# Step input of a state-space scan: scaled by B along the partitions and turned into PSUM, with the sums as accumulating transposes

## Chip, cores and metric

One core of one Trainium2 chip. The metric is device time in microseconds (us) of one execution of the whole program, a decoder layer; smaller is better. TensorE, VectorE, ScalarE, GpSimd and SyncE are PE, DVE, ACT, POOL and SP in the rows.

## What is computed

The change lies in the first of the layer's stages, a selective scan over 32 sequences of 128 tokens with 256 channels and 16 states. Attention, a mixture of experts and a last layer norm follow and stay as they are.

```python
x_dbl = jnp.einsum('bld,ed->ble', hidden_states, W_xproj)   # 64 + 16 + 16 columns
dt_low, Bm, Cm = x_dbl[..., :64], x_dbl[..., 64:80], x_dbl[..., 80:]
delta = softplus(jnp.einsum('blr,dr->bld', dt_low, W_dt) + b_dt)
dA = jnp.exp(delta[..., None] * A)
dBx = (delta * x)[..., None] * Bm[:, :, None, :]
h = dA_t * h + dBx_t                    # for every token t, state n, channel d
y = jnp.einsum('bdn,bn->bd', h, C_t)
x = _layernorm(x + y, axis=-1)
```

## The kernel before

The stage is `scan_phase`. It takes the 32 sequences in 8 groups of 4 (GROUPS, GB), 512 tokens (GT) in a row along the free axis, with the 256 channels as KH = 2 halves of 128 partitions. Inside a group it takes the 16 states one after the other; one state is called a step, so the stage has 128 steps (q = 16 g + n). Each engine has a hand-written program of its own that loops over the groups and steps, and the engines meet at semaphores only.

One step n, with k for the two channel halves:

- ACT, `decays` (L358): decay = exp(A_n * delta), two instructions, made two steps ahead.
- The drive, delta * x * B_n, goes to the PSUM tiles `drive_ps[k]`, one per half. In 12 of 16 steps DVE makes it itself, `drives` (L452): dx from PSUM times `b_sb`, B's row n copied to all 128 partitions. In the steps of POOL_STEPS (2, 6, 9, 14) POOL makes it in SBUF, `make_drive` (L523), and ACT copies it over, `copy_drive` (L366).
- DVE, `scan` (L463): state = decay * previous + drive along the 512 tokens, one instruction per half.
- POOL, `outputs` (L538): hc = state * C_n, both halves in one instruction; C_n is also a row that was copied to all partitions.
- PE, `add_state` (L256), three steps later: y_ps[k] += hc[k], a product with the identity.

SP loads the two broadcast rows of each step (`load_b`, L189, and `load_c`, L196; 128 loads of 256 KB each). State, decay, hc and the rows live in rings of 4 slots (RING), so the scan of step q waits until hc of step q - 4 is made, and a decay waits until the scan four steps back is done.

While one group runs, the next is prepared: PE projects x (`project`, L240 and L242, then `step_size`, L249), ACT takes the parts of the softplus (L333 to L344), POOL adds them to delta (L509) and multiplies by x (L516), ACT copies dx to PSUM (L352). A group's sum comes out with the channels on the partitions; it is copied (`copy_y`, L371), turned by PE (`turn`, L274), and normalised over the channels (DVE L470 and L476, POOL L528 and L531, ACT L384) during the next group.

What sets the order is the code as written, for each engine alone; on ACT a step is:

```python
decays(par, q + 2, n + 2)
if n + 1 in POOL_STEPS:
    copy_drive(g, n + 1)
```

Of the kernel before, what the change touches and what calls it, by code (L numbers as in the profile page):

```python
# [35 lines left out]
POOL_STEPS = (2, 6, 9, 14)  # L36


def merge_moments(dve, stats, stats_ready, stats_count, part, mean, var, done, before):

    even, odd = stats[:, :, 1], stats[:, :, 4]
    dve.wait_ge(stats_ready, stats_count)
    dve.tensor_tensor(part[:, 0, :], even, odd, ALU.add)
    dve.tensor_tensor(part[:, 1, :], even, odd, ALU.subtract)
    dve.tensor_tensor(part[:, 2, :], stats[:, :, 2], stats[:, :, 5], ALU.add).then_inc(done, 1)
    dve.wait_ge(done, 3 * before + 1)
    dve.tensor_scalar(mean[:], part[:, 0, :], 0.5, None, ALU.mult)  # L50
    dve.scalar_tensor_tensor(part[:, 3, :], part[:, 1, :], 0.25, part[:, 1, :], ALU.mult, ALU.mult).then_inc(done, 1)
    dve.wait_ge(done, 3 * before + 2)
    dve.scalar_tensor_tensor(var[:], part[:, 2, :], 1.0 / D, part[:, 3, :], ALU.mult, ALU.add).then_inc(done, 1)
# [20 lines left out]
def scan_phase(nc, x1, ident, xT_dram, w_proj_dram, w_bc_dram, w_dt_dram, b_dt_dram, a_log_dram, bc_dram, attention):  # L74
    with ExitStack() as ctx:
        s = Scope(nc, ctx, "scan")
        w_proj = s.sb("w_proj", [P, KH, R])
        w_bc = s.sb("w_bc", [P, KH, 2 * NS])
        w_dt = s.sb("w_dt", [R, D])
        b_dt = s.sb("b_dt", [P, KH])  # L80
# [4 lines left out]
        rows = s.sb("rows", [2 * NS, GT])  # L85
        dt_low = s.sb("dt_low", [R, GT])
# [3 lines left out]
        z_pos = s.sb("z_pos", [P, KH, GT])  # L90
        delta = [s.sb(f"delta{i}", [P, KH, GB, SEQ]) for i in range(2)]
        dx = [s.sb(f"dx{i}", [P, KH, GT]) for i in range(2)]
        drive = s.sb("drive", [P, KH, GT])
        decay = s.sb("decay", [P, RING, KH, GB, SEQ])
        state = s.sb("state", [P, RING, KH, GT])
        b_sb = s.sb("b_sb", [P, RING, GT])
        c_sb = s.sb("c_sb", [P, RING, GT])
        hc = s.sb("hc", [P, RING, KH, GT])
        yT = s.sb("yT", [P, KH, GT])
        stats = s.sb("stats", [P, GB, 6])  # L100
        moment = s.sb("moment", [P, GB, 2])
        scaled = s.sb("scaled", [P, GB])
        shift = s.sb("shift", [P, GB])
        zero = s.sb("zero", [P, GB])
# [12 lines left out]
        zeroed = s.sem("zeroed")  # L117
        a_ready = s.sem("a_ready")
        proj_ready = s.sem("proj_ready")
        dt_copied = s.sem("dt_copied")  # L120
        rows_ready = s.sem("rows_ready")
        rows_stored = s.sem("rows_stored")
        b_loaded = [s.sem(f"b_loaded{i}") for i in range(RING)]
        c_loaded = [s.sem(f"c_loaded{i}") for i in range(RING)]
        z_ready = s.sem("z_ready")
# [3 lines left out]
        z_pos_ready = s.sem("z_pos_ready")  # L129
        delta_ready = s.sem("delta_ready")  # L130
        dx_ready = s.sem("dx_ready")
        dx_copied = s.sem("dx_copied")
        decay_ready = s.sem("decay_ready")
        drive_ready = s.sem("drive_ready")
        drive_made = s.sem("drive_made")
        drive_copied = s.sem("drive_copied")
        scanned = s.sem("scanned")
        hc_ready = s.sem("hc_ready")
        hc_summed = s.sem("hc_summed")
        y_started = s.sem("y_started")  # L140
        y_copied = s.sem("y_copied")
        turned = s.sem("turned")
        stats_ready = s.sem("stats_ready")
        stats_seen = s.sem("stats_seen")
        mv_ready = s.sem("mv_ready")
        scaled_ready = s.sem("scaled_ready")
        shift_ready = s.sem("shift_ready")
        lv_ready = s.sem("lv_ready")
        rstd_ready = s.sem("rstd_ready")
        normed = s.sem("normed")  # L150
        consts = 4

        def pool_drives(g, n):
            return len(POOL_STEPS) * g + len([x for x in POOL_STEPS if x <= n])

        def dve_drives(g, n):
            return KH * ((STEPS - len(POOL_STEPS)) * g + len([x for x in range(n + 1) if x not in POOL_STEPS]))

        def slot_use(g, n):
            return 16 * (STEPS // RING * g + n // RING + 1)  # L160

        with nc.Block() as block:

            @block.sync
            def _(sp):
                sp.dma_start(w_proj[:], w_proj_dram).then_inc(proj_loaded, 16)
                sp.dma_start(w_bc[:], w_bc_dram).then_inc(proj_loaded, 16)
                sp.dma_start(xT[0][:], xT_dram[:, :, 0:GT]).then_inc(x_loaded[0], 16)
                sp.dma_start(w_dt[:], w_dt_dram).then_inc(const_loaded, 16)
                sp.dma_start(b_dt[:], b_dt_dram).then_inc(const_loaded, 16)  # L170
                sp.dma_start(a_log[:], a_log_dram).then_inc(const_loaded, 16)
                sp.dma_start(ident[0][:], ident[1]).then_inc(const_loaded, 16)

                def store_rows(i, par):
                    g = 2 * i + par
                    sp.wait_ge(rows_ready, g + 1)
                    sp.dma_start(bc_dram[par], rows[:]).then_inc(rows_stored, 16)

                def load_b(i, par, n, first=False):
                    g = 2 * i + par  # L180
                    if n == 0:
                        sp.wait_ge(rows_stored, 16 * (g + 1))
                    if not first:
                        back, m = (g, n - RING) if n >= RING else (g - 1, n - RING + STEPS)
                        if m in POOL_STEPS:
                            sp.wait_ge(drive_made, pool_drives(back, m))
                        else:
                            sp.wait_ge(drive_ready, dve_drives(back, m))
                    sp.dma_start(b_sb[:, n % RING, :], bc_dram[par, n:n + 1, :].broadcast_to([P, GT])).then_inc(b_loaded[n % RING], 16)  # L189

                def load_c(i, par, n):
                    g = 2 * i + par
                    if n == 0:
                        sp.wait_ge(rows_stored, 16 * (g + 1))
                    sp.wait_ge(hc_ready, STEPS * g + n + 1)
                    sp.dma_start(c_sb[:, n % RING, :], bc_dram[par, NS + n:NS + n + 1, :].broadcast_to([P, GT])  # L196
                                 ).then_inc(c_loaded[n % RING], 16)

                def group(i, par, fetch, final=False):
                    g = 2 * i + par  # L200
                    for n in range(STEPS):
                        if n == STEPS - RING - 1 and not final:
                            store_rows(i + par, 1 - par)
                        ahead = n + RING
                        if ahead < STEPS:
                            load_b(i, par, ahead)
                        elif not final:
                            load_b(i + par, 1 - par, ahead - STEPS)
                        ahead = n + RING - 1
                        if ahead < STEPS:  # L210
                            load_c(i, par, ahead)
                        elif not final:
                            load_c(i + par, 1 - par, ahead - STEPS)
# [100 lines left out]
            def _(act):  # L314
# [116 lines left out]
                for n in range(2):  # L431
                    decays(0, n, n)
# [1525 lines left out]
```

## Time and profile before

| | |
|---|---|
| median of 3 timed runs | 1349.92 us (1348.81 to 1350.81) |
| span of the profiled execution, first to last instruction (its own time is given as this span alone) | 1350.7 us |
| first scan starts, last scan starts | 26.0 us, 474.0 us |
| busy in the whole program: PE, DVE, ACT, POOL | 1037.0, 953.6, 713.6, 863.4 us |
| scan stage, 26.0 to 475.2 us: PE, DVE, ACT, POOL busy | 320.00, 413.91, 262.95, 401.78 us of 449.20 |

Busy time of an engine in a stretch counts overlapping instructions once; the mean ns of an instruction is its own length, of which about a tenth of a microsecond overlaps the next where two follow without a wait. A line number is the line of the kernel's source. "Idle before" is how long the engine stood still ahead of an instruction, with the instruction that released it.

### The profile page before, as it was taken

The page shows a single profiled execution, that of the slowest core. Times are in us where ns is not written, and L with a number is a line of the kernel's source. Part 1 is how long each engine was busy: PE and PEld are TensorE (multiplying, and loading weights), DVE is VectorE, ACT ScalarE, POOL GpSimd, SP SyncE. Part 2 cuts the span into 40 slices and gives each one's busy share as a digit, 9 for nine tenths or more (in the row PEclk, how much of TensorE's full clock was granted, in tenths as well). Part 3 has the DMA queues.
Part 4 walks back from the last instruction along what each step waited for, and adds up shares of the span by engine and source line. Part 5 has one row for each costly group of instructions (what it writes and reads, how often), then busy time and mean ns, then how long its engine had stood idle before and what let it go on. Part 6 is the DMA issues. An engine that isn't in the chain of part 4 may idle for free. (4 is left out here: it accounts for less than half of the span.)

```text
span 1350.7 us, 25649 instructions
## 1 busy us (share of the span) xinstructions
PE 1037.0 (77%) x8275; PEld 713.5 (53%) x8275; DVE 953.6 (71%) x1824; ACT 713.6 (53%) x1537; POOL 863.4 (64%) x762
## 2 busy tenths in 40 slices
PE   4877577775767758888888886127999999999980
PEld 1332222322223236666666665026989898999970
DVE  2998999989899947777777875674555555555534
ACT  4565565664656425666666663113555555555433
POOL 4898988989889846777777774405244463464423
PEclk8898998989989869999999997557999999999995
DMA  5454544545444300111111110104243443343317
GB/s 177 149 165 142 176 141 158 169 142 177 144 163 156 127 26 21 45 39 35 35 46 37 35 37 25 70 1 137 48 106 72 115 89 70 103 96 76 40 20 260
DMA packets 80620, 130.71 MB, mean 97 GB/s; under 512 B 12656, under 2 KB 38832, under 8 KB 78512
## 3 DMA queue, kind: packets, MB, share of 16 engines
q1 hardware_dynamic: 68272, 112.91, 25.2%
q0 software_dynamic: 12288, 17.05, 7.8%
q8 instruction: 32, 0.52, 0.2%
q14 instruction: 28, 0.23, 0.1%
HBM read 108.26 MB, written 21.66 MB: 96 GB/s over the span
## 5 line engine op out<-in xcount | busy, mean ns | idle before, releaser
L538 POOL TENSOR_TENSOR scan_hc<-scan_state,scan_c_sb 128x1024 f32<-128x1024 f32 x128 | 298.9, 2356 | 46.8 <-PE scan_y_ps L256 33.9
L463 DVE TENSOR_TENSOR_SCAN scan_state<-scan_decay,scan_drive_ps 128x512 f32<-128x512 f32 x256 | 296.4, 1202 | 33.8 <-ACT scan_drive_ps L366 26.3
L256 PE MATMUL scan_y_ps<-scan_hc,all_ident 128*128 128x512 f32 x524 | 252.8, 623 | 63.4 <-POOL scan_hc L538 63.4
L1624 POOL DMA_INDIRECT acc<-expert_rows,input_lst x64 | 111.2, 1737 | 180.4 <-DVE expert_rows L1753 165.7
L1727 DVE TENSOR_TENSOR expert_hid_lo<-expert_hid,expert_hid_hi 128x512 fp32r<-128x512 f32 x128 | 88.6, 692 | 172.0 <-ACT expert_hid_hi L1711 172.0
L256 PEld LDWEIGHTS scan_y_ps<-scan_hc,all_ident 128*128 128x128 f32 x524 | 96.8, 195 | 212.6 <-POOL scan_hc L538 109.0
L1706 ACT ACTIVATE expert_hid<-expert_h_ps,expert_b 128x512 f32<-128x512 f32 x128 | 88.2, 689 | 189.3 <-PE expert_h_ps L588 187.2
L358 ACT ACTIVATE scan_decay<-scan_delta,scan_a_neg 128x508 f32<-128x508 f32 x256 | 165.0, 710 | 9.4 <-DVE scan_state L463 6.8
L586 PE MATMUL expert_o_ps<-weights_w_hi,expert_hid_hi 128*128 128x256 f32 x512 | 143.9, 281 | 2.2 <-DVE expert_hid_lo L1727 2.2
L588 PE MATMUL expert_o_ps<-weights_w_hi,expert_hid_lo 128*128 128x256 f32 x512 | 143.8, 281 | 0.0
L587 PE MATMUL expert_o_ps<-weights_w_lo,expert_hid_hi 128*128 128x256 f32 x512 | 143.4, 280 | 0.0
L452 DVE TENSOR_TENSOR scan_drive_ps<-scan_dx_ps,scan_b_sb 128x512 f32<-128x512 f32 x192 | 122.1, 682 | 12.0 <-ACT scan_dx_ps L352 12.0
L586 PE MATMUL expert_h_ps<-expert_x_hi,weights_w_hi 128*128 128x512 f32 x256 | 106.6, 416 | 2.4 <-DVE expert_x_lo L1739 2.4
L588 PE MATMUL expert_h_ps<-expert_x_hi,weights_w_lo 128*128 128x512 f32 x256 | 102.1, 399 | 0.0
L587 PE MATMUL expert_h_ps<-expert_x_lo,weights_w_hi 128*128 128x512 f32 x256 | 102.0, 398 | 0.0
L586 PEld LDWEIGHTS expert_o_ps<-weights_w_hi,expert_hid_hi 128*128 128x128 f32 x512 | 96.5, 188 | 8.3 <-issue 2.6
L587 PEld LDWEIGHTS expert_o_ps<-weights_w_lo,expert_hid_hi 128*128 128x128 f32 x512 | 96.6, 189 | 5.9
L588 PEld LDWEIGHTS expert_o_ps<-weights_w_hi,expert_hid_lo 128*128 128x128 f32 x512 | 96.8, 189 | 0.0
L1241 POOL DMA_INDIRECT input_xg<-table,input_lst x64 | 71.4, 1115 | 27.4 <-issue 16.8
L1066 DVE TENSOR_REDUCE attn_top<-attn_s_ps 128x4 bf16<-128x512 f32 x128 | 84.0, 678 | 3.8 <-PE attn_s_ps L839 3.7
L1711 ACT ACTIVATE expert_hid_hi<-expert_hid 128x512 fp32r<-128x512 f32 x128 | 79.5, 621 | 0.6
L366 ACT ACTIVATE scan_drive_ps<-scan_drive 128x512 f32<-128x512 f32 x64 | 37.2, 600 | 75.9 <-DVE scan_state L463 75.9
(215 smaller groups left out, 2327.2 us busy)
## 6 DMA issues: line engine op xcount, KB each, us to landing
scan_b_sb<-rows SPq DMA_DIRECT2D x128, 256.0 KB, 3.6
scan_c_sb<-rows SPq DMA_DIRECT2D x128, 256.0 KB, 3.4
weights_w<-w SPq DMA_DIRECT2D x16, 1024.0 KB, 5.2
table<-all_row SPq DMA_DIRECT2D x32, 132.0 KB, 1.7
scan_xT<-xT SPq DMA_DIRECT2D x8, 512.0 KB, 4.5
attn_ctxT<-ctxT SPq DMA_DIRECT2D x32, 128.0 KB, 2.4
acc<-all_row SPq DMA_DIRECT2D x32, 128.0 KB, 1.7
final_a<-acc SPq DMA_DIRECT2D x8, 512.0 KB, 6.6
```

Of the source, the lines that this page charges most:

```text
L256: last = pe.matmul(y_ps[k][:], ident[0][:], hc[:, n % RING, k, :], start=False, stop=(n == NS - 1))
L358: act.activation(decay[:, n % RING, k, :, 1:SEQ], delta[par][:, k, :, 1:SEQ], ACT.Exp, scale=a_neg[:, k, n:n + 1]).then_inc(decay_ready, 1)
L452: dve.tensor_tensor(drive_ps[k][:], dx_ps[k][:], b_sb[:, n % RING, :], ALU.mult).then_inc(drive_ready, 1)
L463: dve.tensor_tensor_scan(state[:, n % RING, k, :], decay[:, n % RING, k, :, :].rearrange("p b t -> p (b t)"), drive_ps[k][:], 0.0, ALU.mul ...
L538: pool.tensor_tensor(hc[:, n % RING, :, :], state[:, n % RING, :, :], c_sb[:, n % RING, :].unsqueeze(1).broadcast_to([P, KH, GT]), ALU.mul ...
L586: pe.matmul(out, a_hi, b_hi, start=start and n == 0, stop=False, skip_group_check=True)
L587: pe.matmul(out, a_hi, b_lo, start=False, stop=False, skip_group_check=True)
L588: last = pe.matmul(out, a_lo, b_hi, start=False, stop=stop and n == len(pairs) - 1, skip_group_check=True)
L1066: dve.tensor_reduce(top[:, j, 0:4], s_ps[j][:].rearrange("p (h k) -> p h k", k=P), AX.X, ALU.max).then_inc(m["top_done"], 1)
L1624: pool.indirect_dma_start(out=acc_dram, out_offset=bass.IndirectOffsetOnAxis(ap=lst[h.parity][:, n:n + 1], axis=0), in_=rows[h.part][:, t, ...
L1706: act.activation(hid[:, f % 2, :], h_ps[f % 2][:], ACT.Gelu, bias=b1[h.parity][:, f:f + 1]).then_inc(gelu_done, 1)
L1727: dve.tensor_tensor(hid_lo[:, f % RING_H, :], hid[:, f % 2, :], hid_hi[:, f % RING_H, :].bitcast(F32), ALU.subtract).then_inc(hid_ready, 1)
```

## The change

The stage is rewritten in the following places; the steps, groups, rings, decays, scans and products with C stay.

1. dx (delta * x) is no longer copied to PSUM. PE turns it once per group (`turn_dx`), ACT copies the result to SBUF as `dxT`: tokens on the partitions, the 256 channels of a sequence along the free axis. B is turned the same way (`turn_b`, `copy_b`) to `bT`, one number per token and state.
2. In every step the drive is then dxT times a number per partition: `scale_dx`, four instructions of 128x256. ACT makes 12 of 16 steps (ACT_STEPS), POOL the steps 3, 7, 11, 15.
3. PE turns the scaled tile back into the two PSUM tiles, four 128x128 transposes per half (`fill`), and DVE scans from there. DVE's products and ACT's copies of the drive are gone, and so are the 128 loads of B.
4. The sums over the states: `add_state` and `start_y` are transposes too, which add up in PSUM, so that a group's sum comes out with tokens on the partitions. `copy_y` and `turn` are gone, and there are two sets of sum tiles, one per group parity.
5. W_xproj is one matrix of 96 columns, b_dt is a row of `w_dt` against a row of ones, and delta (relu and add) and dx move from ACT and POOL to DVE (`step_sizes`, `step_inputs`). The layer norm's shift moves from POOL to DVE.

The core of the diff:

```diff
-POOL_STEPS = (2, 6, 9, 14)
+POOL_STEPS = (3, 7, 11, 15)
+ACT_STEPS = tuple(n for n in range(STEPS) if n not in POOL_STEPS)
...
+                def turn_dx(grp, half):
+                    pe.wait_ge(dx_ready, grp.g + 1)
+                    for j in range(2):
+                        for k in range(KH):
+                            c = j * D + k * P
+                            b = 2 * half + j
+                            last = pe.transpose(m_ps[half][:, c:c + P], dx[:, k, b * P:(b + 1) * P], ident[0][:])
+                    last.then_inc(dx_turned, 1)
...
+                def fill(p, k):
...
+                    since(pe, scanned, KH * (p.q - 1) + k + 1)
                     for j in range(GB):
+                        last = pe.transpose(drive_ps[k][:, j * P:(j + 1) * P], scaled[:, p.slot, j, k * P:(k + 1) * P], ident[0][:])
+                    last.then_inc(filled, 1)
+
+                def add_state(p, half):
+
+                    if half == 0:
+                        pe.wait_ge(hc_ready, p.q + 1)
+                    for j in range(2):
                         for k in range(KH):
...
+                            last = pe.matmul(y_ps[p.par][half][:, c:c + P], hc[:, p.slot, k, b * P:(b + 1) * P], ident[0][:],
+                                             start=False, stop=(p.n == STEPS - 1), is_transpose=True, skip_group_check=True)
...
+                        for half in range(2):
+                            if grp.at(n + 1) is not None:
+                                fill(grp.at(n + 1), half)
+                            if grp.at(n - LAG) is not None:
+                                add_state(grp.at(n - LAG), half)
+                            if not grp.final:
+                                prepare(grp.plus_one(), n, half)
...
+                def scale_dx(p):
+
+                    if p.n == ACT_STEPS[0]:
+                        act.wait_ge(dxT_ready, 2 * (p.g + 1))
+                        act.wait_ge(b_copied, p.g + 1)
+                    since(act, filled, KH * (p.q - RING + 1))
+                    for j in range(GB):
+                        last = act.activation(scaled[:, p.slot, j, :], dxT[p.par][:, j, :], ACT.Copy, scale=bT[p.par][:, j, p.n:p.n + 1])
+                    last.then_inc(scaled_by_act, 1)
...
-                        dve.tensor_tensor(drive_ps[k][:], dx_ps[k][:], b_sb[:, n % RING, :], ALU.mult).then_inc(drive_ready, 1)
...
+                    dve.wait_ge(filled, KH * p.q + k + 1)
+                    dve.wait_ge(decay_ready, KH * p.q + k + 1)
...
+                def step_sizes(grp, k):
+                    if k == 0:
+                        dve.wait_ge(z_log_ready, grp.g + 1)
+                    dve.scalar_tensor_tensor(delta[grp.par][:, k, :, :].rearrange("p b t -> p (b t)"), m_ps[k][:], 0.0, z_log[:, k, :],
+                                             ALU.max, ALU.add).then_inc(delta_ready, 1)
...
+                        last = pool.tensor_scalar(scaled[:, p.slot, j, :], dxT[p.par][:, j, :], bT[p.par][:, j, p.n:p.n + 1], None, ALU.mult)
```

The order of instructions shows the change at three places (a trailing digit of a name is the buffer's number).

On DVE, step 3 of the first group, before:

```order
L451 ISA
L452 TENSOR_TENSOR scan_drive0_ps<-scan_dx0_ps,scan_b_sb 128x512
L451 REGISTER_ALU
L452 TENSOR_TENSOR scan_drive1_ps<-scan_dx1_ps,scan_b_sb 128x512
L461 ISA
L463 SCALAR_TENSOR_TENSOR scan_state<-scan_decay,scan_drive0_ps 128x512
L463 SCALAR_TENSOR_TENSOR scan_state<-scan_decay,scan_drive1_ps 128x512
```

and DVE now, steps 11 and 12, the only ones of a group with more than scans besides the layer norm:

```order
L455 SCALAR_TENSOR_TENSOR scan_state<-scan_decay,scan_drive0_ps 128x512
L461 SCALAR_TENSOR_TENSOR scan_delta1<-scan_m0_ps,scan_z_log 128x512
L455 SCALAR_TENSOR_TENSOR scan_state<-scan_decay,scan_drive1_ps 128x512
L461 SCALAR_TENSOR_TENSOR scan_delta1<-scan_m1_ps,scan_z_log 128x512
L455 SCALAR_TENSOR_TENSOR scan_state<-scan_decay,scan_drive0_ps 128x512
L467 TENSOR_TENSOR scan_dx<-scan_delta1,scan_xT1 128x1024
L455 SCALAR_TENSOR_TENSOR scan_state<-scan_decay,scan_drive1_ps 128x512
```

The pair of products ahead of the scans is gone from DVE, and the three instructions that make the next group's delta and dx have come to it, between the two scans of a step.

On ACT now, from the step in which it copies the projection to the second absolute value of the softplus (decays and scalings are made two steps ahead):

```order
L376 ACTIVATE scan_decay<-scan_delta0,scan_a_neg 128x4x127 x2
L345 ACTIVATE scan_proj<-scan_m0_ps 96x512
L376 ACTIVATE scan_decay<-scan_delta0,scan_a_neg 128x4x127 x2
L386 ACTIVATE scan_scaled<-scan_dxT0,scan_bT0 128x256 x4
L376 ACTIVATE scan_decay<-scan_delta0,scan_a_neg 128x4x127 x2
L386 ACTIVATE scan_scaled<-scan_dxT0,scan_bT0 128x256 x4
L350 ACTIVATE scan_bT1<-scan_m1_ps 128x64
L376 ACTIVATE scan_decay<-scan_delta0,scan_a_neg 128x4x127 x2
L386 ACTIVATE scan_scaled<-scan_dxT0,scan_bT0 128x256 x4
L355 ACTIVATE scan_z_abs<-scan_m0_ps 128x512
L376 ACTIVATE scan_decay<-scan_delta0,scan_a_neg 128x4x127 x2
L355 ACTIVATE scan_z_abs<-scan_m1_ps 128x512
```

Four scalings (L386) follow the two decays in each of ACT's own steps; steps of POOL's, the first and the last here, have the decays alone, and the preparation's work is spread between them.

On PE now, two halves of a step with the next group's step size (L248) in it:

```order
L281 MATMUL scan_drive0_ps<-all_ident,scan_scaled 128x128 x4
L292 MATMUL scan_y00_ps<-all_ident,scan_hc 128x128 x4
L248 MATMUL scan_m0_ps<-scan_proj,scan_w_dt 128x256
L281 MATMUL scan_drive1_ps<-all_ident,scan_scaled 128x128 x4
L292 MATMUL scan_y01_ps<-all_ident,scan_hc 128x128 x4
```

Where PE had two products of 128x512 per step, it now has sixteen transposes of 128x128, eight of which DVE's next scans wait for.

## Rows read from the trace of the kernel before

**Rows 1.** Busy time by stretch: the scan stage, 30 us of it, the choosing stage
```profile
core 0: us, PE busy (x) PEld busy (x) DVE busy (x) ACT busy (x) POOL busy (x), PEclk, DMA share, GB/s
26.00:475.20 449.20, 320.00 (x686) 119.42 (x687) 413.91 (x512) 262.95 (x449) 401.78 (x189) 0.91 0.48 155
187.00:217.00 30.00, 20.73 (x52) 8.10 (x50) 28.77 (x38) 18.95 (x33) 30.00 (x14) 1.00 0.54 174
846.00:906.00 60.00, 9.01 (x52) 6.28 (x53) 44.15 (x210) 7.81 (x20) 13.18 (x22) 0.50 0.11 40
```
**Rows 2.** Groups by line, 24 to 478 us, DVE: busy, mean ns | idle before
```profile
L463 DVE TENSOR_TENSOR_SCAN scan_state<-scan_decay,scan_drive_ps 128x512 f32<-128x512 f32 x256 | 296.4, 1202 | 33.8 <-ACT scan_drive_ps L366 26.3 <-issue 5.2 <-ACT scan_decay L358 2.3
L452 DVE TENSOR_TENSOR scan_drive_ps<-scan_dx_ps,scan_b_sb 128x512 f32<-128x512 f32 x192 | 122.1, 682 | 12.0 <-ACT scan_dx_ps L352 12.0
L470 DVE BATCH_NORM_STATS2 scan_stats<-scan_m_ps 128x6 f32<-128x256 f32 x32 | 11.2, 413 | 0.1
L476 DVE BATCH_NORM_AGGREGATE scan_moment<-scan_stats 128x2 f32<-128x6 f32 x32 | 3.0, 158 | 1.4 <-DVE scan_stats L470 1.4
```
**Rows 3.** Timeline around 250 us: runs without a wait (start us, length us)
```profile
239.58 0.73 ACT L358 ACTIVATE scan_decay<-scan_delta,scan_a_neg 128x508 f32<-128x508 f32 x1
...
241.13 2.54 ACT L358 ACTIVATE scan_decay<-scan_delta,scan_a_neg 128x508 f32<-128x508 f32 x4
...
246.45 1.27 DVE L452 TENSOR_TENSOR scan_drive_ps<-scan_dx_ps,scan_b_sb 128x512 f32<-128x512 f32 x2
...
254.46 4.54 DVE L463 TENSOR_TENSOR_SCAN scan_state<-scan_decay,scan_drive_ps 128x512 f32<-128x512 f32 x4
...
255.38 9.30 POOL L538 TENSOR_TENSOR scan_hc<-scan_state,scan_c_sb 128x1024 f32<-128x1024 f32 x4
...
279.11 1.93 ACT L384 ACTIVATE front_x<-scan_m_ps,scan_shift,scan_rstd 128x256 f32 x4 [6.19 <-POOL scan_shift L531]
```
**Rows 4.** Groups by line, ACT, 24 to 478 us: work that goes or stays
```profile
L366 ACT ACTIVATE scan_drive_ps<-scan_drive 128x512 f32<-128x512 f32 x64 | 37.2, 600 | 75.9 <-DVE scan_state L463 75.9
L333 ACT ACTIVATE scan_z_abs<-scan_m_ps,scan_b_dt 128x512 f32<-128x512 f32 x14 | 9.6, 689 | 13.8 <-PE scan_m_ps L249 13.8
L352 ACT ACTIVATE scan_dx_ps<-scan_dx 128x512 f32<-128x512 f32 x16 | 8.9, 590 | 10.2 <-POOL scan_dx L516 10.2
L338 ACT ACTIVATE scan_z_exp<-scan_z_abs 128x1024 f32<-128x1024 f32 x7 | 7.5, 1073 | 0.0
L377 ACT ACTIVATE scan_ln_var<-scan_moment,scan_eps 128x4 f32<-128x4 f32 x8 | 2.4, 298 | 0.4 <-DVE scan_moment L476 0.2
```
**Rows 5.** Groups by line, whole program: the nearest instructions to the new ones
```profile
L1213 ACT ACTIVATE weights_w_hi<-weights_w 128x256 fp32r<-128x256 f32 x128 | 50.6, 406 | 8.1 <-DMA weights_w<-w 8.1
L1711 ACT ACTIVATE expert_hid_hi<-expert_hid 128x512 fp32r<-128x512 f32 x128 | 79.5, 621 | 0.6
L754 POOL TENSOR_SCALAR all_row<-attn_res,attn_o_mv,attn_o_rstd 128x256 f32<-128x256 f32 x32 | 39.1, 1223 | 57.3 <-ACT attn_o_rstd L995 57.3
L721 POOL CAST attn_ctx_hi<-attn_ctxT 128x256 fp32r<-128x256 f32 x32 | 12.8, 399 | 3.6 <-DMA attn_ctxT<-ctxT 1.8 <-PE attn_kv_ps L588 1.8
L1870 POOL TENSOR_SCALAR final_o<-final_a,final_rstd,final_shift 128x256 f32<-128x256 f32 x16 | 8.8, 559 | 17.5 <-DVE final_shift L1835 17.4
L1161 DVE TENSOR_TENSOR xattn_w_kv_lo<-xattn_w_kv,xattn_w_kv_hi 128x1024 fp32r<-128x1024 f32 x1 | 1.2, 1215 | 0.0
```
**Rows 6.** Groups by line, POOL, 24 to 478 us: work that goes
```profile
L523 POOL TENSOR_TENSOR scan_drive<-scan_dx,scan_b_sb 128x1024 f32<-128x1024 f32 x32 | 75.4, 2355 | 0.2
```
**Rows 7.** Timeline, PE alone: bursts of transposes and of products
```profile
266.20 1.04 PE L274 MATMUL scan_m_ps<-all_ident,scan_yT 128*128 128x128 f32 x8
...
201.62 1.98 PE L256 MATMUL scan_y_ps<-scan_hc,all_ident 128*128 128x512 f32 x4 [2.62 <-POOL scan_hc L538]
...
281.09 3.62 PE L240 MATMUL scan_m_ps<-scan_xT,scan_w_bc 128*32 128x512 f32 x4 [7.44 <-ACT front_x L384]
...
898.77 1.11 PE L1370 MATMUL choose_turn_ps<-all_ident,choose_part_f 128*128 128x128 f32 x4 [2.09 <-DVE choose_part_f L1463]
```

More of the change, by code:

```diff
@@ L35 @@
 LAG = 3
-POOL_STEPS = (2, 6, 9, 14)
[L39 to L53, printed above, removed]
+POOL_STEPS = (3, 7, 11, 15)
+ACT_STEPS = tuple(n for n in range(STEPS) if n not in POOL_STEPS)
+PROJ = R + 2 * NS
 class Scope:
@@ L174, in store_rows @@
[L174 to L213, printed above, removed]
-                        if n == STEPS - 2 and fetch:
-                            sp.wait_ge(y_started, g + 1)
-                            sp.wait_ge(dx_ready, g + 1)
-                            sp.dma_start(xT[par][:], xT_dram[:, :, ds((g + 2) * GT, GT)]).then_inc(x_loaded[par], 16)
@@ L229, in _ @@
[L229 to L230 removed]
+                groups(sp, group)
             @block.tensor
             def _(pe):
[L234 to L243 removed]
@@ L311, in _ @@
-                last.then_inc(turned, 1)
+                    fill(Group(0, 0).at(0), k)
+                groups(pe, group)
+                for n in range(STEPS - LAG, STEPS):
+                    for half in range(2):
+                        add_state(Group(GROUPS // 2 - 1, 1).at(n), half)
             @block.scalar
@@ new lines, in _ @@
+                act.wait_ge(const_loaded, 16 * consts)
+                act.activation(a_exp[:], a_log[:], ACT.Exp).then_inc(a_exp_ready, 1)
+                act.wait_ge(set_up, 3)
+                for n in range(STEPS):
+                    prepare(Group(0, 0), n)
+                act.wait_ge(a_ready, 1)
+                for n in range(2):
+                    decays(Group(0, 0).at(n))
+                    if n in ACT_STEPS:
+                        scale_dx(Group(0, 0).at(n))
+                groups(act, group)
@@ L467, in statistics, with scan @@
-                def statistics(g):
-                    dve.wait_ge(turned, g + 2)
-                    for j in range(GB):
-                        last = dve.bn_stats(stats[:, j, :], m_ps[j // 2][:, (j % 2) * D:(j % 2 + 1) * D])
+                def scan(p, k):
+                    if k == 0:
+                        since(dve, hc_ready, p.q - RING + 1)
+                    dve.wait_ge(filled, KH * p.q + k + 1)
+                    dve.wait_ge(decay_ready, KH * p.q + k + 1)
+                    dve.tensor_tensor_scan(state[:, p.slot, k, :], decay[:, p.slot, k, :, :].rearrange("p b t -> p (b t)"),
+                                           drive_ps[k][:], 0.0, ALU.mult, ALU.add).then_inc(scanned, 1)
@@ L575, in scan_phase @@
+                groups(pool, group)
         return s.sems
@@ L602, in plus @@
         return Seq(self.pair, self.offset + n)
-def since(eng, sem, count):
-    if not (isinstance(count, int) and count < 1):
-        eng.wait_ge(sem, count)
 def attention_phase(nc, x1, ident, gate_all, const, ctxT_dram, table_dram, acc_dram, choice, row, row_stored, finished):
```

615 lines of the change are left out of this document (286 added, 329 removed).

## The prediction

> **What bounds the kernel now.** The change stays inside the scan stage, so I first read busy time by stretch. Between the first scan's start and the last scan's end, 449.2 us, DVE works 413.91 us, POOL 401.78, PE 320.00 and ACT 262.95 [rows 1]. DVE is the fullest, so I next read its groups by line: 256 scans and 192 products that make the drive, 122.1 us [rows 2]. The same rows say what ends the 35.3 us (449.20 - 413.91) in which DVE stands still: mostly ACT's copy of a drive that POOL made (26.3 us). ACT, in turn, stood 75.9 us in front of those copies waiting for a scan [rows 4]. The stage is thus DVE's work plus a loop DVE, ACT, DVE at POOL's steps. POOL is close behind, with 32 drives of 2.36 us (75.4 us) besides its 128 products with C [rows 3, 6]. The change takes work from DVE and gives it to ACT, PE and, in smaller portions, POOL. The question is which of the four is fullest afterwards. For that I need the price of an instruction in an unbroken run, which the timeline shows better than a mean: a scan 4.54 / 4 = 1.135 us, a product with C 9.30 / 4 = 2.325, a decay (2.54 - 0.73) / 3 = 0.603 after the first [rows 3].
>
> **DVE.** It loses the 192 products (122.1 us). It keeps 256 x 1.135 = 291 us of scans and 11.2 + 3.0 of statistics [rows 2]. Per group it gains two instructions for delta, priced as the pair of products at 1.27 [rows 3], and one of 128x1024 for dx, 1.215 [rows 5]; for the seven groups that are prepared inside the stage that is 17 us. Sum: 322 us. DVE is no longer the bound.
>
> **ACT.** It loses the 64 copies of drives (37.2 us) with their wait, the copies of dx (8.9 us) and one of two softplus parts of the shape of L333 [rows 4]. It gains 96 x 4 = 384 scalings of 128x256 with a number per partition. The trace has no such instruction. The nearest is the decay, which also reads SBUF, writes SBUF and takes a number per partition: 0.603 for 508 elements. Two plain copies give the price of an element, (621 - 406) / 256 = 0.84 ns [rows 5], so 252 elements fewer take off 0.212: 0.39 us, or 150 us in all. From below, the plain copy's 0.406 less the 0.127 by which a decay in a run is shorter than a single one: 0.28, or 107 us. From above, the normalisation of the same width with two such numbers, 1.93 / 4 = 0.483 [rows 3], or 185 us. I take 0.39, since the decay differs in its length only. Decays stay: 256 x 0.603 = 154 us. Per group there remain the copies of the projection, of B and of dxT (0.59 + 0.3 + 2 x 0.59), two absolute values (1.38), exponential and logarithm (2 x 1.07), variance and root (0.6) and the normalisation (1.93) [rows 3, 4]: 8.1 us, 65 in all, of which about 8 lie before the first scan or behind the last. That makes 154 + 150 + 57 = 361 us. One new wait sits on ACT: it copies dxT only when DVE has made dx and PE has turned it, and the next group's first scaling is queued behind that copy. DVE reaches dx in step 12 and ACT the copy in its step 13, so I take 1 us per group, 7 in all: 368 us.
>
> **POOL.** It loses its 32 drives (75.4 us) and two sums per group of the same shape, 16 x 2.36 = 38 us [rows 6]. It keeps 128 x 2.325 = 298 us and gains 32 x 4 = 128 scalings of 128x256. Three rows bound one: 0.399 us for a cast of that shape, 0.559 and 1.223 us for an instruction of the same name with two operations [rows 5]. I take 0.559: it multiplies, as the new one does, while the dear one subtracts first. 128 x 0.559 = 72, so POOL has 369 us. The ends: 349 us and 454 us.
>
> **PE.** Sixteen transposes per step take the place of two products. At the full clock eight of them took 1.04 us [rows 7], so 2.08 per step, 266 in all. Preparing a group takes two products' worth of columns twice (2 x 1.98 us [rows 7]), sixteen transposes (2.08) and four narrow ones (0.5 at most): 6.6, seven times 46. Sum: 312 us. More matters than the sum, since DVE's scans now wait for PE. A half's four transposes (0.52 us) can start when the scan of that half is done, and the scan of the other half, 1.135 us, covers them and the 0.52 of sums behind them. Where a piece of preparation of about 0.5 follows, PE comes some 0.4 late, in up to 14 of a group's 32 half steps; ACT's and POOL's pace of 2.9 us per step leaves 0.6 of slack against DVE's 2.27, so I cost this at nothing while the clock is full. If PE waits at the sums for POOL's product, the next fill is queued behind it and DVE stands; that again is POOL's pace.
>
> **SP and DMA.** 128 loads of B go; the DMA share of 0.48 [rows 1] falls. Nothing in the rows of DVE waits for a load, so this is worth nothing.
>
> **The sum.** POOL with 369 and ACT with 368 are equal, and a stage does not run at its fullest engine's sum: DVE, the fullest, stood 35.3 us of it. The worst of that loop is gone, but two equally full engines with bursts (POOL's four scalings, ACT's preparation) take its place, so I take half, 17 us, between 0 and 35. The stage then takes 386 us instead of 449.2, a gain of 63. Ahead of the first scan and behind the last the chains change by pieces of a microsecond or two in both directions (a turn more ahead, a copy and a turn less behind); I take 0. The profiled execution's span of 1350.7 becomes 1287.5; it lies 0.8 above the median of the three runs, so the forecast is **1287**. Its own range: ACT's dearer scaling gives 403 + 17 = 420 us, hence 1321; POOL's cheaper one with ACT's cheaper one 349 + 17 = 366 us, hence 1267, and a little less with less friction. So 1262 to 1321.
>
> **Rival one, slower: PE at its lower clock.** The mechanism is PE's pace between the scan of a half and the next. PE has two levels, 2.4 and 1.2 GHz (granted 1.00 and 0.50). After 7.4 us without work four passes took 3.62 us where 1.98 is usual [rows 7], a factor of 1.83. In the choosing stage, where PE is busy 9 of 60 us at a granted clock of 0.50 [rows 1], four transposes took 1.11 us against 0.52. At 1.83 times, PE's 312 us become 571; since part of the burst times is a tail that the next burst overlaps, 520 to 571. That is a total of 1420 to 1472, and 1446 in the middle. It decides from 386 / 312 = 1.24 times the present price, and the kernel is slower than before from 449 / 312 = 1.44. Against it: with 20.7 us of work in 30, PE kept the full clock throughout, with gaps of 2.6 us [rows 1, 7], and the new stage gives PE 2.4 us of work in every 3 us, without the long gaps. For it: that work was products, while the new stream is nearly all transposes, and no row shows the clock of a stretch with transposes alone. The Trainium skill (TensorE: Matmul & The Clock Gate, Part 4: PE-mode transpose) says that the full clock does not engage for transpose mode, because it does not count as PE-busy in the same way; by that rule this rival is the outcome and its 1446 the time. The L274 row shows transposes running at the full clock right behind products, which neither bears the rule out nor refutes it. I give this rival 0.12. If PE falls to the lower level for part of the stage only, somewhat over a quarter of it, the time lies between 1321 and 1345; 0.07.
>
> **Rival two, not faster: POOL's scaling at the dear price.** With 1.223 us each POOL has 454 us, with friction up to 471, and the total is 1355 to 1372. It decides from (449 - 17 - 298) / 128 = 1.05 us per scaling. For it, the name of the instruction and the number per partition; against it, the subtraction. 0.08, of which 0.02 ends within 0.2% of the time before.
>
> **Rival three, faster still.** ACT at 0.28 and POOL at 0.399 with little friction: 349 us, about 1250. 0.05.
>
> **How the numbers follow.** The forecast has 0.68. Faster by over 0.2% (about what a measurement of this kernel can tell from no change) are the forecast, rival three and the partly lower clock: 0.80. Within 0.2%: 0.02. Slower: 0.12 + 0.06 = 0.18. The range from 1250 to 1345 takes in the forecast's own, rival three and the partly lower clock, 0.80 together; beyond it lie the two slow rivals.
>
> **What would show it.** Right: the span of the 256 scans near 386 us; scans of 1.2 us mean; ACT's group of 384 scalings near 150 us busy; POOL's of 128 near 72; POOL and ACT over 90% busy in the stage and DVE below 90%; transposes at 0.13 us each in runs and a granted clock near 1.00. Wrong: DVE's idle time put down to PE's `drive_ps` with a clock near 0.50 (rival one); a POOL scaling over 1 us (rival two); idle time on both ACT and POOL at the turn of a group, each waiting for the other through DVE, which would mean that my friction is too small.

## The result and the profile after

The changed kernel takes 1335.14 us (median of four runs, 1334.65 to 1339.98) against 1350.37 for the kernel before it (1348.81 to 1352.51): a ratio of 0.989, 95% interval 0.987 to 0.991. It is faster by 15 us. The forecast was 1287, faster by 63: the sign was right and the size four times too large. The profiled execution spans 1338.2 us.

| | before | after |
|---|---|---|
| first scan's start to last scan's end | 449.2 us | 434.0 us |
| from there to the program's end | 875.5 us | 876.4 us |

The change lies in the stage, as assumed; the first scan starts 1.8 us later than before. Busy time by stretch, after: the stage, then the first 340 us of the attention (the columns are those of [rows 1]: PE, PEld, DVE, ACT, POOL busy, granted clock, DMA share, GB/s).

```profile
27.80:461.80 434.00, 327.17 (x2271) 277.28 (x2270) 370.68 (x341) 357.08 (x731) 411.49 (x250) 0.90 0.27 83
461.80:801.80 340.00, 279.09 (x4559) 213.11 (x4556) 253.28 (x569) 208.46 (x612) 235.79 (x375) 0.97 0.11 35
```

POOL is the fullest engine now: 411.5 of 434.0 us, where 369 was forecast. DVE has 370.7 instead of 322. ACT (357) and PE (327) are near their forecasts of 361 and 312. The groups by line between 26 and 470 us say which instructions made the difference (busy, mean ns of one | idle before):

```profile
L541 POOL TENSOR_TENSOR scan_hc<-scan_state,scan_c_sb 128x1024 f32<-128x1024 f32 x128 | 299.3, 2372 | 22.5 <-PE scan_drive_ps L281 16.4 <-DVE scan_state L455 6.1
L455 DVE TENSOR_TENSOR_SCAN scan_state<-scan_decay,scan_drive_ps 128x512 f32<-128x512 f32 x256 | 295.0, 1200 | 47.3 <-PE scan_drive_ps L281 35.3 <-issue 10.3
...
L386 ACT ACTIVATE scan_scaled<-scan_dxT,scan_bT 128x256 f32<-128x256 f32 x382 | 161.9, 498 | 0.0
...
L534 POOL TENSOR_SCALAR scan_scaled<-scan_dxT,scan_bT 128x256 f32<-128x256 f32 x126 | 121.3, 985 | 0.0
L486 DVE SCALAR_TENSOR_TENSOR scan_shift<-scan_moment,scan_rstd 128x4 f32<-128x4 f32 x7 | 44.3, 6330 | 0.0
L467 DVE TENSOR_TENSOR scan_dx<-scan_delta,scan_xT 128x1024 f32<-128x1024 f32 x7 | 15.8, 2255 | 0.0
...
L368 ACT ACTIVATE scan_dxT<-scan_m_ps 128x512 f32<-128x512 f32 x14 | 8.3, 591 | 10.7 <-PE scan_m_ps L258 10.7
```

Two rows stand out. POOL's scalings (L534) take 121.3 us instead of 72: 0.985 us each. And the layer norm's shift (L486), four numbers per partition, takes DVE 6.33 us each time, 44.3 us in all. The timeline of one group shows what happens around it (start us, length us; runs without a wait are one row):

```profile
259.12 3.66 POOL L534 TENSOR_SCALAR scan_scaled<-scan_dxT,scan_bT 128x256 f32<-128x256 f32 x4
...
260.19 1.69 ACT L386 ACTIVATE scan_scaled<-scan_dxT,scan_bT 128x256 f32<-128x256 f32 x4
...
262.71 7.00 POOL L541 TENSOR_TENSOR scan_hc<-scan_state,scan_c_sb 128x1024 f32<-128x1024 f32 x3
...
263.29 6.45 DVE L486 SCALAR_TENSOR_TENSOR scan_shift<-scan_moment,scan_rstd 128x4 f32<-128x4 f32 x1
...
265.22 0.60 PE L248 MATMUL scan_m_ps<-scan_proj,scan_w_dt 97*128 97x256 f32 x2
270.92 1.12 PE L281 MATMUL scan_drive_ps<-all_ident,scan_scaled 128*128 128x128 f32 x4 [5.11 <-DVE scan_state L455]
271.83 1.06 PE L292 MATMUL scan_y_ps<-all_ident,scan_hc 128*128 128x128 f32 x4
...
272.05 2.37 POOL L541 TENSOR_TENSOR scan_hc<-scan_state,scan_c_sb 128x1024 f32<-128x1024 f32 x1 [2.34 <-PE scan_drive_ps L281]
```

The shift starts at 263.29, in the first of three products with C that POOL makes without a pause, and ends at 269.74, when that run ends (262.71 + 7.00 = 269.71). Until then DVE scans nothing; PE has nothing to fill for 5.11 us; and POOL, once its products are used up, finds no new state and stands for 2.34 us. All seven shifts inside the stage end within 0.1 us of the end of such a run; the eighth, after POOL's last product, took 0.163 us. So the fullest engine is stopped seven times by an instruction that it delays itself: 7 x 2.34 = 16.4 us, the share in the L541 row above. PE pays too: its four transposes took 1.12 us after the pause instead of 0.66, the price of its lower level, until 276.9.

### The profile page after: what moved, and what is told of

Same layout as the page of the kernel before. It is cut to its first block and busy times, and to the rows that moved or that the text cites. A ratio compares the mean times of both kernels' runs of the same rounds, so it can differ in the third digit from the quotient of the medians.

```text
span 1338.2 us, 28802 instructions
## 1 busy us (share of the span) xinstructions
PE 1039.9 (78%) x9883; PEld 874.9 (65%) x9883; DVE 914.6 (68%) x1657; ACT 806.0 (60%) x1817; POOL 868.6 (65%) x822
## 5 line engine op out<-in xcount | busy, mean ns | idle before, releaser
L541 POOL TENSOR_TENSOR scan_hc<-scan_state,scan_c_sb 128x1024 f32<-128x1024 f32 x128 | 299.3, 2372 | 22.5 <-PE scan_drive_ps L281 16.4
L281 PE MATMUL scan_drive_ps<-all_ident,scan_scaled 128*128 128x128 f32 x1024 | 178.9, 303 | 102.0 <-DVE scan_state L455 59.8
L281 PEld LDWEIGHTS scan_drive_ps<-all_ident,scan_scaled 128*128 128x128 f32 x1024 | 126.3, 153 | 148.4 <-DVE scan_state L455 92.3
L376 ACT ACTIVATE scan_decay<-scan_delta,scan_a_neg 128x508 f32<-128x508 f32 x256 | 168.2, 710 | 12.8 <-DVE scan_state L455 12.8
L292 PE MATMUL scan_y_ps<-all_ident,scan_hc 128*128 128x128 f32 x1024 | 164.7, 288 | 2.6 <-POOL scan_hc L541 2.4
L386 ACT ACTIVATE scan_scaled<-scan_dxT,scan_bT 128x256 f32<-128x256 f32 x384 | 162.7, 498 | 0.0
L534 POOL TENSOR_SCALAR scan_scaled<-scan_dxT,scan_bT 128x256 f32<-128x256 f32 x128 | 123.1, 984 | 23.7 <-ACT scan_dxT L368 23.7
L292 PEld LDWEIGHTS scan_y_ps<-all_ident,scan_hc 128*128 128x128 f32 x1024 | 130.8, 150 | 3.3 <-POOL scan_hc L541 3.3
```

Source lines behind the costliest of these rows:

```text
L281: last = pe.transpose(drive_ps[k][:, j * P:(j + 1) * P], scaled[:, p.slot, j, k * P:(k + 1) * P], ident[0][:])
L292: last = pe.matmul(y_ps[p.par][half][:, c:c + P], hc[:, p.slot, k, b * P:(b + 1) * P], ident[0][:], start=False, stop=(p.n == STEPS - 1), ...
L376: act.activation(decay[:, p.slot, k, :, 1:SEQ], delta[p.par][:, k, :, 1:SEQ], ACT.Exp, scale=a_neg[:, k, p.n:p.n + 1]).then_inc(decay_read ...
L386: last = act.activation(scaled[:, p.slot, j, :], dxT[p.par][:, j, :], ACT.Copy, scale=bT[p.par][:, j, p.n:p.n + 1])
L534: last = pool.tensor_scalar(scaled[:, p.slot, j, :], dxT[p.par][:, j, :], bT[p.par][:, j, p.n:p.n + 1], None, ALU.mult)
L541: pool.tensor_tensor(hc[:, p.slot, :, :], state[:, p.slot, :, :], c_sb[:, p.slot, :].unsqueeze(1).broadcast_to([P, KH, GT]), ALU.mult).the ...
```

## The experiments

The theory was that POOL sets the stage, by two things that the forecast lacked: a scaling costs it 0.92 us in a run (3.66 / 4), and the shift stops the loop. The rivals were that the round trip scan, PE, scan sets the pace, that the 6.3 us of the shift are only a wait that is booked as work, and that POOL's price belongs to the place and not to the instruction. Stage below means first scan's start to last scan's end.

**One product on POOL instead of four scalings.** It makes the same values.

```diff
-for j in range(GB):
-    last = pool.tensor_scalar(scaled[:, p.slot, j, :], dxT[p.par][:, j, :], bT[p.par][:, j, p.n:p.n + 1], None, ALU.mult)
-last.then_inc(scaled_by_pool, 1)
+pool.tensor_tensor(scaled[:, p.slot, :, :], dxT[p.par][:],
+                   bT[p.par][:, :, p.n:p.n + 1].broadcast_to([P, GB, D]), ALU.mult).then_inc(scaled_by_pool, 1)
```

> POOL's four scalings of 128x256 in its own steps (3.66 us in a run) become one tensor_tensor of 128x1024 against B broadcast along the row; the values are the same. Theory (POOL's price per scaling, 0.92 us instead of the forecast 0.56, sets the stage): the product with C has that shape and takes 2.33 us, so POOL loses 32 x 1.33 = 43 us; the changed kernel's 1335 becomes 1292 (1287 to 1305, the upper end if ACT is next). Rival (the round trip scan, turn on PE, scan sets the pace, and POOL only follows it): 1330 to 1337.

Measured: 1279.74 us (1276.61 to 1284.86), ratio 0.948 (0.944 to 0.952). Busy time in the stage:

```profile
27.50:404.10 376.60, 312.99 (x2272) 262.76 (x2271) 341.22 (x341) 354.03 (x731) 358.03 (x157) 0.95 0.32 96
```

and two groups by line:

```profile
L533 POOL TENSOR_TENSOR scan_scaled<-scan_dxT,scan_bT 128x1024 f32<-128x1024 f32 x31 | 66.0, 2128 | 0.0
L486 DVE SCALAR_TENSOR_TENSOR scan_shift<-scan_moment,scan_rstd 128x4 f32<-128x4 f32 x8 | 19.0, 2373 | 1.0 <-ACT scan_rstd L393 1.0
```

The round trip through PE as the bound is refuted: PE's part was not touched, and the stage lost 57 us. It lost more than the 43 expected, and the time lies below its range. POOL's work fell by 53.5 us (411.5 to 358.0), since a step's scaling takes 2.13 us instead of four times 0.985; and the shift, which was not touched either, fell from 6.33 to 2.69 us for the seven inside the stage (the row's 2.37 counts the eighth, of 0.16, as well): four of them took 1.5 us, three 3.9 to 5.1. So the two costs are coupled: the shift waits long where POOL is late. With POOL's scaling at a price near the 0.56 that the forecast had used, the kernel came out at 1280, beside the 1287 that was forecast.

**The shift with one operand from PSUM.** ACT writes the inverse deviation a second time, to a PSUM bank that is free at that moment (PE's step size for the first half moves half a step).

```diff
+act.activation(m_ps[0][:, 0:GB], ln_var[:], ACT.Exp, scale=-0.5).then_inc(rstd_ready, 1)
...
-dve.scalar_tensor_tensor(shift[:], moment[:, :, 0], -1.0, rstd[:], ALU.mult, ALU.mult).then_inc(shift_ready, 1)
+dve.scalar_tensor_tensor(shift[:], moment[:, :, 0], -1.0, m_ps[0][:, 0:GB], ALU.mult, ALU.mult).then_inc(shift_ready, 1)
```

> The layer norm's shift stays on DVE at the same place, but reads the inverse deviation from PSUM (ACT writes it there a second time, 0.2 us per group), so that one operand of two lies in SBUF; PE's step size for the first half moves half a step later to leave the bank free. Theory (the shift, with both operands in SBUF, stands 6.2 us on DVE until POOL runs out of work, and POOL then idles 2.34 us): the shift takes 0.2 us, POOL's 7 x 2.34 = 16.4 us of idle time go, 1335 becomes 1319 (1312 to 1322). Rival (the 6.2 us are a wait for ACT's inverse deviation that the trace books as work): the shift stays near 6 us and the time at 1335.

Measured: 1318.18 us (1316.34 to 1322.28), ratio 0.977 (0.974 to 0.980). Busy time in the stage, and groups by line:

```profile
27.40:440.30 412.90, 324.05 (x2268) 278.74 (x2267) 345.86 (x341) 355.52 (x738) 409.34 (x250) 0.91 0.29 87
...
L544 POOL TENSOR_TENSOR scan_hc<-scan_state,scan_c_sb 128x1024 f32<-128x1024 f32 x128 | 299.1, 2372 | 3.6 <-DVE scan_state L458 3.4
...
L470 DVE TENSOR_TENSOR scan_dx<-scan_delta,scan_xT 128x1024 f32<-128x1024 f32 x7 | 31.5, 4501 | 0.0
...
L489 DVE SCALAR_TENSOR_TENSOR scan_shift<-scan_moment,scan_m_ps 128x4 f32<-128x4 f32 x8 | 1.1, 136 | 0.7 <-ACT scan_m_ps L396 0.7
```

The same instruction, released by the same engine at the same place, takes 0.136 us: what it waited for was not ACT; the wait comes with the second operand in SBUF. POOL's idle time fell from 22.5 to 3.6 us, and the stage, 412.9 us, is now POOL's work (409.3) and little else. The wait did not vanish altogether: it went to the other DVE instruction with two operands in SBUF, the product for dx (L470), 4.5 us each instead of 2.26. There it costs POOL less, since the scans that POOL needs next are already made.

**Both.**

> The two edits together: one product on POOL, and the shift with one operand from PSUM. If the two costs are separate they add: 1335 - 43 - 16 = 1276. If ACT (361 us of work in the stage and waits of its own) becomes the bound first: 1280 to 1295. If the round trip through PE sets the pace: 1320 or more.

Measured: 1271.74 us (1271.13 to 1274.64), ratio 0.942 (0.940 to 0.945), a stage of 368.9:

```profile
27.40:396.30 368.90, 308.93 (x2270) 258.53 (x2269) 325.79 (x341) 354.10 (x737) 355.57 (x157) 0.96 0.31 98
```

Alone the two edits gave 57.4 and 21.1 us in the stage, together 65.1: less than their sum, as it must be if one of them already shortens what the other removes. The time is a little below the 1276 of two separate costs only because the one product alone had given more than was expected.

**POOL's scalings as multiply and add.** Does the price belong to the pair of operations?

```diff
-last = pool.tensor_scalar(scaled[:, p.slot, j, :], dxT[p.par][:, j, :], bT[p.par][:, j, p.n:p.n + 1], None, ALU.mult)
+last = pool.tensor_scalar(scaled[:, p.slot, j, :], dxT[p.par][:, j, :], bT[p.par][:, j, p.n:p.n + 1], zero[:, 0:1], ALU.mult, ALU.add)
```

`zero` is a new tile, one zero per partition.

> POOL keeps four tensor_scalars per step of its own, but each is a multiplication and an addition of a zero per partition, the pair that took 0.559 us in the final stage; the values are the same. Theory (POOL's price goes by the pair of operations: multiply and add 0.56, subtract and multiply 1.22, multiply alone 0.92): the scaling falls to 0.56 us and 1335 becomes 1335 - 128 x 0.36 = 1289 (1284 to 1305). Rival one (the price belongs to this place, where POOL works beside DVE and ACT): 0.92 us and 1335. Rival two (an operation costs some 0.3 us each): 1.22 us and 1374.

Measured: 1314.88 us (1313.08 to 1317.69), ratio 0.974 (0.971 to 0.977). Groups by line:

```profile
L543 POOL TENSOR_TENSOR scan_hc<-scan_state,scan_c_sb 128x1024 f32<-128x1024 f32 x128 | 299.5, 2364 | 34.8 <-DVE scan_state L456 20.6 <-PE scan_drive_ps L282 14.1
...
L536 POOL TENSOR_SCALAR scan_scaled<-scan_dxT,scan_bT,scan_zero 128x256 f32<-128x256 f32 x125 | 74.4, 609 | 0.0
L487 DVE SCALAR_TENSOR_TENSOR scan_shift<-scan_moment,scan_rstd 128x4 f32<-128x4 f32 x8 | 32.2, 4030 | 1.0 <-ACT scan_rstd L394 1.0
```

and busy time by stretch, the stage and the first 340 us of the attention after it:

```profile
27.80:426.70 398.90, 328.30 (x2271) 277.25 (x2270) 356.58 (x341) 355.31 (x730) 365.71 (x250) 0.89 0.29 91
426.70:766.70 340.00, 277.86 (x4372) 212.49 (x4370) 243.96 (x545) 200.63 (x589) 228.07 (x363) 0.93 0.11 35
```

The price does go by the pair: with an addition more, each scaling takes 0.609 us instead of 0.985 (four in a run 2.17 us instead of 3.66), and POOL's work fell by 46 us. Rivals one and two of this run are refuted. But the time missed its expectation of 1289 by 26. Some 11 of these are behind the stage: from the last scan to the choosing stage the profile has 388.3 us instead of 377.3, at a granted clock of 0.93 instead of 0.97. Another 11 are in the stage, where 35 of the 46 us arrived: POOL idles 34.8 us, and the shift still takes 4.6 us for the seven inside the stage. The rest lies in the comparison, since the changed kernel's profiled execution, at 1339.98, is itself 5 us above its median.

**The same with the shift from PSUM.**

> Multiply and add on POOL (0.54 us per scaling in a run) together with the shift that reads PSUM. Alone the first gave 1314.9 where 1289 was expected. If the shift's wait (32 us on DVE in that run) and a slower attention behind the stage are what was missing, the stage here comes to that of the one product with the same shift, 369 us and a few more for the 8 us that POOL's scalings are longer: 1272 to 1285. If four short instructions on POOL hold DVE up more than one long one does: 1295 or more.

Measured: 1289.67 us (1284.34 to 1296.43), ratio 0.952 (0.948 to 0.956). The stage and the first 340 us of the attention:

```profile
27.80:403.20 375.40, 312.80 (x2267) 262.87 (x2266) 327.29 (x341) 354.80 (x737) 365.24 (x250) 0.96 0.32 96
403.20:743.20 340.00, 278.46 (x4300) 212.70 (x4299) 239.59 (x536) 196.19 (x577) 224.18 (x356) 0.91 0.11 34
```

The time lies above the 1272 to 1285 of the theory and below the rival's 1295. The stage decides for the theory: it is 375.4 us, 6.5 above that of the run with both edits, for 9.7 us more of POOL's work, so the shift was what the stage lacked in the run before. The profiled execution is 25 us longer than that run's (the medians 18); 17 of the 25 lie again in the attention (394.2 us against 377.3), which nothing in the edit touches, at a clock of 0.91. Why its clock is lower after these two kernels was not found.

**Two steps of sixteen for POOL.** One constant, in the changed kernel.

```diff
-POOL_STEPS = (3, 7, 11, 15)
+POOL_STEPS = (7, 15)
```

> The changed kernel with one constant changed: POOL scales in the steps 7 and 15 alone, ACT in the other fourteen. Theory (POOL's work with its price of 0.92 us per scaling sets the stage): POOL loses 16 x 3.66 = 59 us and ACT gains 16 x 1.65 = 26, so ACT is next with some 385 us, and the stage falls from 434 to about 395: 1296 (1285 to 1308). Rival (the shift's wait alone costs the stage its time): 1330 to 1337.

Measured: 1303.84 us (1299.41 to 1306.06), ratio 0.963 (0.959 to 0.967).

```profile
26.00:425.90 399.90, 324.14 (x2271) 275.21 (x2270) 333.89 (x341) 379.73 (x794) 356.78 (x190) 0.90 0.30 90
```

As expected: POOL has 55 us less, and ACT, with 379.7 of 399.9 us, is next. The shift was left as it is. Where POOL is not the late engine it is short: six of the seven inside the stage take 0.8 to 0.9 us, and the last, behind 1.36 us in which DVE waited for ACT, takes 5.12, to the end of a run of three products.

**dx after the turn.** A version without the second collision, on top of both edits: PE turns delta, and DVE multiplies it out of PSUM by x, which is loaded once more for that with tokens on the partitions.

```diff
-pe.transpose(m_ps[half][:, c:c + P], dx[:, k, b * P:(b + 1) * P], ident[0][:])
+pe.transpose(m_ps[half][:, c:c + P], delta[grp.par][:, k, b, :], ident[0][:])
...
-act.activation(dxT[grp.par][:, 2 * half:2 * half + 2, :].rearrange("p j d -> p (j d)"), m_ps[half][:],
-               ACT.Copy).then_inc(dxT_ready, 1)
...
-dve.tensor_tensor(dx[:], delta[grp.par][:].rearrange("p k b t -> p k (b t)"), xT[grp.par][:], ALU.mult).then_inc(dx_ready, 1)
...
+dve.tensor_tensor(dxT[grp.par][:, 2 * half:2 * half + 2, :].rearrange("p j d -> p (j d)"), m_ps[half][:],
+                  x1[:, ds(GB * grp.g + 2 * half, 2), :].rearrange("p j d -> p (j d)"), ALU.mult).then_inc(dxT_ready, 1)
```

> On top of one product on POOL and the shift from PSUM (1271.7): PE turns delta instead of dx, and DVE multiplies the turned delta, from PSUM, by x with tokens on the partitions (loaded into the place of the result), straight into dxT. So DVE's product has one operand in SBUF instead of two, and ACT's copy of dxT is gone. Theory (a DVE instruction with both operands in SBUF and POOL's instructions hold each other up): the product takes 2 x 0.68 us instead of 2.2, POOL's scaling behind it is no longer 2.9 but 1.9 us, ACT loses 9 us: 1262 (1257 to 1267). Rival (that wait is covered): 1271.

Measured: 1267.36 us (1261.85 to 1270.66), ratio 0.935 (0.931 to 0.939). Busy time in the stage, and groups by line:

```profile
25.20:387.40 362.20, 311.52 (x2271) 262.88 (x2270) 319.64 (x348) 347.84 (x723) 350.27 (x157) 0.95 0.35 108
...
L531 POOL TENSOR_TENSOR scan_scaled<-scan_dxT,scan_bT 128x1024 f32<-128x1024 f32 x31 | 59.2, 1909 | 0.0
...
L464 DVE TENSOR_TENSOR scan_dxT<-scan_m_ps,front_x 128x512 f32<-128x512 f32 x14 | 9.6, 683 | 2.5 <-PE scan_m_ps L261 2.1
```

Both prices came as expected (0.683 us, and POOL's scaling 1.91 where its mean with the other dx had been 2.10), and the stage fell by 6.7 us to 362.2. The total fell by 4.4 only and ends just above its range: in the profiled execution the attention, whose code the edit leaves alone, took 4 us of the gain back (381.4 us against 377.3).

**Diagonals on POOL.** In POOL's steps, now five of sixteen, POOL multiplies the identity by B, half the elements, and PE makes the drive as a product.

```diff
-POOL_STEPS = (3, 7, 11, 15)
+POOL_STEPS = (3, 6, 9, 12, 15)
...
+if p.n in POOL_STEPS:
+    last = pe.matmul(drive_ps[k][:, j * P:(j + 1) * P], dxT[p.par][:, j, k * P:(k + 1) * P], scaled[:, p.slot, j, 0:P],
+                     start=True, stop=True)
...
+pool.tensor_tensor(scaled[:, p.slot, :, 0:P], ident[0][:].unsqueeze(1).broadcast_to([P, GB, P]),
+                   bT[p.par][:, :, p.n:p.n + 1].broadcast_to([P, GB, P]), ALU.mult).then_inc(scaled_by_pool, 1)
```

> On top of the kernel with dx after the turn: in POOL's steps, now five of sixteen (3, 6, 9, 12, 15), POOL scales the identity instead of dxT (four diagonals, one product of 128x512, about 1.1 us) and PE makes the drive as a product of dxT with the diagonal instead of a transpose. POOL 298 + 40 x 1.15 = 344 us, ACT 150 of decays + 146 of scalings + 49 = 345, PE 307 + 40 x 8 x 0.11 = 342. If the three run as close to full as before: stage 355, 1254 (1245 to 1262). If PE's products come too late for the scan: 1265 or more.

Measured: 1259.63 us (1255.97 to 1261.19), ratio 0.930 (0.927 to 0.934), inside its range and the fastest version.

```profile
26.30:383.20 356.90, 330.95 (x2594) 293.73 (x2594) 322.09 (x348) 336.53 (x692) 334.88 (x166) 0.98 0.36 110
```

All four engines now work 322 to 337 of 356.9 us; there is no single bound left to move work away from.

## Why the prediction was right and wrong

**What bounds the kernel before, and the method: right.** The stage is bound by its fullest engine and a friction, and the sum by engines told which one that would be. Put the measured price into the prediction's own sum: 298 + 32 x 3.66 = 415 us for POOL (411.5 measured), with its 17 of friction 432 (434.0 measured), and a total of 1333 (1335.14 measured). That it comes out so close is in part luck, since the friction had another reason than the forecast gave.

**POOL: the step that failed.** "I take 0.559: it multiplies, as the new one does, while the dear one subtracts first." The new instruction is neither of the two: it has one operation, and took 0.92 us in a run. The 72 us of that term measured 121.3. Of the 48 us by which the stage missed its 386, 42.5 are POOL's busy time (411.5 against 369) and 5.5 its idle time (22.5 against 17). Between rows as far apart as 0.40 and 1.22, nearness in the operation was the wrong guide: fewer operations were not cheaper. A forecast could have known the safe form: the tensor_tensor of L523 and L538 in [rows 3, 6] bounds the same elements by 2.36 us per step, and the run with one product took 2.13.

**DVE: a moved instruction was not costed.** The change's fifth item moves the shift to DVE, and the prediction gives DVE the products for delta and dx alone. By its size nothing was missed, since it takes 0.163 us by itself; in the stage it took 44.3 us. What should have been asked is what the new DVE instructions share with POOL: before, no DVE instruction in the stage had two operands in SBUF. The same holds for dx, priced at 1.215 from a row where POOL was idle and measured at 2.26. 322 + 44 + 7 = 373, measured 370.7.

The trace of before had a hint of such a wait, just behind its stage, which the prediction did not use. A cast on DVE, from SBUF to SBUF with one operand, stood through POOL's last product:

```profile
475.34 2.38 POOL L538 TENSOR_TENSOR scan_hc<-scan_state,scan_c_sb 128x1024 f32<-128x1024 f32 x1 [0.99 <-issue]
475.44 2.84 DVE L1153 CAST xattn_w_kv_hi<-xattn_w_kv 128x1024 fp32r<-128x1024 f32 x1
```

In the changed kernel the casts come in this order:

```profile
461.73 5.49 DVE L1124 CAST xattn_w_q_hi<-xattn_w_q 128x512 fp32r<-128x512 f32 x1
467.14 0.68 DVE L1124 CAST xattn_w_kv_hi<-xattn_w_kv 128x1024 fp32r<-128x1024 f32 x1
467.74 0.41 DVE L1124 CAST xattn_w_o_hi<-xattn_w_o 128x512 fp32r<-128x512 f32 x1
```

The first falls beside POOL's last products, which end at 466.9; the other two find POOL idle. So two operands in SBUF are not the only form that waits; what sets the casts apart from the scans, which run beside POOL without such a wait, was not tested.

The Trainium skill (SBUF — State Buffer, Who interferes with whom) says that a DVE instruction with two SBUF inputs and a GpSimd instruction that reads SBUF exclude each other, and that whichever starts first keeps the other out. By that rule the shift would wait for one product, up to 2.4 us. The kind of instruction agrees (6.33 us with both operands in SBUF, 0.136 with one in PSUM); the length does not: in this kernel it waited through products of POOL that followed without a pause, to the end of the run.

**Friction: 17 forecast, 22.5 us of POOL's idle time measured, for another reason.** It was thought to come from bursts; 16.4 of it is the seven pauses after the shift.

**ACT and PE: about right.** A scaling on ACT in a run is 1.69 / 4 = 0.42 us where 0.39 was taken; ACT's 357 us stand beside 361, and its new wait, at the copy of dxT (L368), is 10.7 us where 7 was taken. PE's 327 us beside 312 hold stretches at the lower level, after the pauses; with both edits PE works 308.9 us.

**Rival one, PE at its lower clock: refuted as the outcome.** The timeline of PE shows the usual stretch of the new stage, with transposes alone:

```profile
260.09 0.66 PE L281 MATMUL scan_drive_ps<-all_ident,scan_scaled 128*128 128x128 f32 x4
260.58 0.60 PE L292 MATMUL scan_y_ps<-all_ident,scan_hc 128*128 128x128 f32 x4
261.20 0.66 PE L281 MATMUL scan_drive_ps<-all_ident,scan_scaled 128*128 128x128 f32 x4
261.69 0.60 PE L292 MATMUL scan_y_ps<-all_ident,scan_hc 128*128 128x128 f32 x4
```

Four transposes start 0.49 us after the four before them (260.09, 260.58), the pace of the full clock (1.04 us for eight in [rows 7]). A stretch in which PE has transposes and nothing else has the granted clock 1.00:

```profile
286.00:297.50 11.50, 9.38 (x72) 7.72 (x72) 11.50 (x12) 10.70 (x23) 11.24 (x7) 1.00 0.23 59
```

The mean granted clock of the stage is 0.90, and 0.96 in the run with both edits. The rule of the Trainium skill that was weighed there (TensorE: Matmul & The Clock Gate, Part 4: PE-mode transpose) would have had these transposes at the lower level; the trace disagrees. In small, the mechanism is there: after each pause at the shift the bursts take 1.06 to 1.12 us, for some 3 to 6 us.

**Rival two, POOL's dear price: half of what happened.** The price, 0.92 in a run and 0.985 on average, lies between the forecast's 0.56 and the rival's 1.22, a little below the 1.05 from which that rival decides; so the kernel is still faster, but barely.

## What to carry to other kernels

Price an instruction of GpSimd by a row of exactly its form, operations included; where there is none, use a form that the trace prices, here one product with a broadcast operand. Before work moves to DVE, look where its operands lie: with two of them in SBUF, here, even four numbers stood for 6.33 us beside a busy GpSimd, and one operand in PSUM took that away (0.136). And when two engines stop each other, take out the load on the late one first: that shortened the wait as well (from 6.33 to 2.69 us here).

## What was not expected of the hardware

- One operation more made GpSimd's tensor_scalar faster: a run of four of 128x256 took 3.66 us as a multiplication and 2.17 as multiplication and addition; one tensor_tensor over the same elements 1.91 in the version with dx after the turn.
- A DVE instruction with two operands in SBUF waited 6.33 us on average, to the end of GpSimd's run of products. Where GpSimd was less late some of them got in between two products of a run that went on: four of seven with one product (1.5 us each), six of seven with two steps of sixteen (0.8 to 0.9). Why the others do not get in stays open.
- Transposes alone held PE at the full clock (1.00 from 286.0 to 297.5 us).
- In two versions the attention, the same code in all, ran at a granted clock of 0.93 and 0.91 instead of 0.95 to 0.97, and 11 and 17 us longer. The cause stays open.
